# Flamingo block with mixture of experts on one core: tiled attention and scores, first rows loaded first, and a reordered second normalisation

## The reference

```python
x = x + tanh(g_xattn[0]) * xattn(layernorm(x), ctx_512, Wq, Wkv_expand, Wout)
x = x + tanh(g_ffn[0]) * ffn(layernorm(x), gate_w, w1, w2, w3, ws1, ws2, ws3)
# xattn: 16 heads of 32; scores * 1/sqrt(32), where(tril(512 x 64)), softmax over 64 keys, attn @ v, @ Wout.T
# ffn: shared expert (silu(x ws1) * (x ws3)) ws2 for every row, plus the best 2 of 8 experts, weighted by
#      softmax(x gate_w), each (silu(x w1[e]) * (x w3[e])) w2[e], inner width 256
```

## Time and profile before

| | |
|---|---|
| time, median of 3 runs (lowest, highest) | 488.65 us (487.75, 490.65) |
| time of the profiled execution | 488.76 us |
| its span, first to last instruction | 487.0 us |
| mean granted TensorE clock | 0.981 of full |
| HBM read, written | 35.54 MB, 22.70 MB |
| copy of one tile's scores (ScalarE, L713, two instructions) | 1.25 us |
| VectorE row maximum or row sum of a tile (L1088, L1094); reciprocal (L1097) | 1.21 us; 0.25 us |
| ScalarE and VectorE parts of one half of the shared weights | 1.47 us; 1.75 us |
| VectorE low part of the query weights | 2.28 us |
| ScalarE normalisation of a tile (L688), fill of kbd (4 instructions) | 0.80 us, 2.58 us |

### The profile page before, as it was taken

How to read it: one execution, slowest core, us unless ns; L and a number is a source line. 1 busy time by engine, 2 the same in 40 slices (tenths; PEclk the granted TensorE clock), 3 DMA queues, 4 the chain that set the end, 5 groups by cost and what they waited for, 6 DMA issues and landing times.

```text
span 487.0 us, 7654 instructions
## 1 busy us (share of the span) xinstructions
PE 427.6 (88%) x2445; PEld 231.1 (47%) x2446; DVE 307.9 (63%) x659; ACT 249.9 (51%) x450; POOL 230.0 (47%) x205
## 2 busy tenths in 40 slices
PE   2599789998999989988897979889999999999981
PEld 1355435554555555554444435445455545544540
DVE  4788876888568885688767868963334334333330
ACT  3879565767537675376342526743343434343330
POOL 4007527541875417749152041855546455565422
PEclk9999989999999999999998899999999999999996
DMA  7920023241042253541642375866557656576453
GB/s 305 416 69 1 0 66 126 92 153 65 2 131 86 88 194 24 173 153 67 232 193 71 107 228 167 185 122 105 116 95 125 113 102 125 88 128 104 90 66 43
DMA packets 20478, 58.61 MB, mean 120 GB/s; under 512 B 3489, under 2 KB 3745, under 8 KB 19810
## 3 DMA queue, kind: packets, MB, share of 16 engines
q0 software_dynamic: 9504, 20.48, 23.7%
q1 hardware_dynamic: 10946, 37.77, 22.9%
HBM read 35.54 MB, written 22.70 MB: 120 GB/s over the span
## 4 chain that ended last, share of the span: by engine, by line
PE 66%; DVE 15%; ACT 6%; issue 5%; POOL 3%; DMA 3%; POOLq 0%; SPq 0%; DVEq 0%; ACTq 0%
PE bank L1554 56%; PE bank L1559 9%; ACT arena L656 4%; DVE arena L987 3%; DVE xn L1056 2%; POOL arena L555 2%; DVE x_sb L1034 1%; DMA xrows<-xn 1%; DVE mx L1094 1%; DMA rows<-xrows,entry 1%; DVE mv L1002 1%; DMA arena<-in_wkv 1%; POOL lists L533 1%; ACT arena L688 1%; DVE mx L1088 1%
## 5 line engine op out<-in xcount | busy, mean ns | idle before, releaser
L1554 PE MATMUL bank<-arena 128*128 128x512 f16 (+1 forms) x576 | 109.5, 347 | 3.4 <-DVE arena L987 1.6
L1554 PE MATMUL bank<-arena,GT 128*128 x468 | 107.4, 379 | 2.2 <-issue 2.0
L640 POOL DMA_INDIRECT out<-rows,entry x39 | 61.7, 1582 | 80.8 <-ACT rows L962 29.9
L1554 PE MATMUL bank<-arena,gT 128*128 (+1 forms) x330 | 80.2, 379 | 2.2 <-DVE gT L986 1.8
L1554 PEld LDWEIGHTS bank<-arena 128*128 128x128 f16 x576 | 55.9, 98 | 51.7 <-issue 3.9
L656 ACT ACTIVATE arena<-bank 128x512 f16<-128x512 f32 (+1 forms) x88 | 49.4, 586 | 47.8 <-PE bank L1554 29.1
L1554 PEld LDWEIGHTS bank<-arena,GT 128*128 128x128 f16 x468 | 45.8, 98 | 49.0 <-issue 2.9
L987 DVE SCALAR_TENSOR_TENSOR arena<-bank,arena 128x512 f16<-128x512 f32 (+1 forms) x72 | 45.8, 666 | 22.2 <-ACT arena L656 21.8
L616 POOL DMA_INDIRECT rows<-xrows,entry x39 | 39.3, 1008 | 37.0 <-DVE entry L1362 20.3
L986 DVE TENSOR_TENSOR GT<-bank,GT 128x512 f16<-128x512 f32 x39 | 26.9, 690 | 46.4 <-ACT GT L656 46.3
L1554 PE MATMUL bank<-arena,x2T 128*128 128x512 f16 x192 | 46.6, 395 | 4.1 <-DVE x2T L986 4.1
(11 more groups left out here) (169 smaller groups left out, 590.2 us busy)
## 6 DMA issues: line engine op xcount, KB each, us to landing
x_sb<-in_experts SPq DMA_DIRECT2D x9, 768.0 KB, 5.1
rows<-in_experts SPq DMA_DIRECT2D x6, 768.0 KB, 5.7
xrows<-xn SPq DMA_DIRECT2D x16, 256.0 KB, 2.4
out<-x_sb SPq DMA_DIRECT2D x16, 256.0 KB, 2.2
image<-GT SPq DMA_DIRECT2D x5, 768.0 KB, 4.1
arena<-image SPq DMA_DIRECT2D x10, 384.0 KB, 5.3
x_sb<-in_x SPq DMA_DIRECT2D x2, 1024.0 KB, 8.8
x_sb<-in_x SPq DMA_DIRECT2D x1, 2048.0 KB, 16.3
```

Of the source, the lines that this page charges most:

```text
L640: nc.gpsimd.indirect_dma_start(out=out, out_offset=bass.IndirectOffsetOnAxis(ap=entry[:, 1, j:j + 1], axis=0), in_=Y[:, j % RING, :], in_o ...
L1554: last = nc.tensor.matmul(dst, a, b, start=n == 0, stop=n == len(steps) - 1)
```

## The change

Loads come in another order: the first two tiles of rows, the next two, then the query weights in two halves, then the context. VectorE normalises the first batch itself (`first_norm`); ScalarE did. Keys are made between the second and the third query projection, in the banks of scores and turned tiles.

`scores` uses 64 partitions (2 heads) per matmul, alternately the lower and the upper half, each half with its own bank, 24 matmuls of 128 columns per tile. `attend` takes the values where they lie, 64 keys by 32 columns per head, and writes each head to its own 32 output partitions: 48 matmuls of 512 columns per batch. vbd, its memset and `fill_v` go. `scores` waits until both halves of the previous tile are copied.

The turn of normalised tile 0 moves from the feed-forward to between the third and fourth output projection, and in the feed-forward the hidden products and the last scores change places. On GpSimd the image subtractions move behind later steps, and `softmax_sub` 2 comes after the second `power2`. On VectorE `head_max` 0 goes ahead of `make_x1` 0, the router's placement and `head_sum` 2 ahead of the mix, and shared weights, gate and aggregates of the start move. ScalarE's list follows.

```diff
-        kbd = part(NG * GH * SK, F16)
+        kbd = part(NG * 2 * SK, F16)
+        part(NG * 2 * SK)
         S = part(PER * NH * SK)
...
-        vbd = sb("vbd", [P, 2 * PR * P], F16)
...
-        wqv = wq_s.rearrange("p (h c n) -> p h c n", h=2, c=DC)
+        wqv = wq_s.rearrange("p (h g c n) -> p h g c n", h=2, g=NG, c=DC)
...
-        vbdv = vbd[:, :].rearrange("p (h r m) -> p h r m", h=2, r=PR)
...

-        MIX_FIRST = (("q", 0), ("q", 1), ("v", 0), ("q", 2), ("v", 1), ("q", 3), ("p", 0), ("v", 2), ("p", 1),
-                     ("v", 3), ("p", 2), ("p", 3))
+        MIX_FIRST = (("q", 0), ("q", 1), ("v", 0), ("q", 2), ("p", 0), ("v", 1), ("q", 3), ("p", 1), ("v", 2),
...
             return () if isinstance(b, int) and b == B - 1 else MIX
+
+        def wq_half(n, low=0):
+
+            return slice((2 * low + n) * (DC * D // 2), (2 * low + n + 1) * (DC * D // 2))
+
+        def keys_bank(g):
+
+            return (score_bank + turn_bank)[g][:, 0:B * SK]
+
+        def pair_of(g, j):
+
+            return j // 2 * NG + g
...

         @block.sync
         def _(sp):
+            for n in range(2):
+                sp.dma_start(x_sb[:, 2 * n * D:2 * (n + 1) * D].rearrange("p (t d) -> p t d", t=2),
+                             x[:, 2 * n:2 * (n + 1), :]).then_inc(ld_x0[n], 16)
+            for n in range(2):
+                sp.dma_start(wq_raw[:, wq_half(n)], wq[:, wq_half(n)]).then_inc(ld_wq[n], 16)
             sp.dma_start(ctx_raw.rearrange("p (b e k) -> p b e k", b=B, e=2), ctx_rows).then_inc(ld_kv, 16)
             sp.dma_start(wkv_raw, wkv).then_inc(ld_kv, 16)
-            sp.dma_start(x_sb[:, 0:PER * D].rearrange("p (t d) -> p t d", t=PER), x[:, 0:PER, :]).then_inc(ld_x0, 16)
-            sp.dma_start(gl[:, 0:2], gates).then_inc(ld_gates, 16)
-            sp.dma_start(wq_raw, wq).then_inc(ld_wq, 16)
             sp.dma_start(x_sb[:, PER * D:2 * PER * D].rearrange("p (t d) -> p t d", t=PER),
                          x[:, PER:2 * PER, :]).then_inc(ld_x1, 16)
...
             pool.memset(kbd.bitcast(F32), 0.0).then_inc(consts, 1)
-            pool.memset(vbd[:, :].bitcast(F32), 0.0).then_inc(consts, 1)
             pool.iota(first_high[:, :], pattern=[[-1, E]], base=E, channel_multiplier=0,
...
                     split_piece(0)
-                elif prev is not None:
-                    image_rest(2 * b - 1)
                 for i in range(PER):
                     if not nxt and i == 3:
                         split_piece(1)
+                    if nxt and prev is not None and i == 2:
+                        image_rest(2 * b - 1)
                     softmax_mul(b, i)
...
                     scatter_pairs(prev, (0,))
                 if nxt:
                     softmax_mask(b + 1)
-                    image_rest(2 * b)
                     softmax_sub(b + 1, 0)
                 power2(b, 0)
                 if nxt:
                     softmax_sub(b + 1, 1)
-                    softmax_sub(b + 1, 2)
+                    image_rest(2 * b)
                 else:
                     scatter_pairs(prev, (1,))
                 power2(b, 1)
+                if nxt:
+                    softmax_sub(b + 1, 2)

...
-                    last = hi(kbdv[rows, :, :, n * SK:(n + 1) * SK],
+                    last = hi(kbdv[rows, :, :, n % 2 * SK:(n % 2 + 1) * SK],
...
+            def wq_high(n):
+                act.wait_ge(ld_wq[n], 16)
+                hi(wq_s[:, wq_half(n)], wq_raw[:, wq_half(n)], S_W).then_inc(wq_hi, 1)
...
                 c = f + 1
-                turn_hi(c, "x2", 0)
+                turn_hi(c, "x2", 1)
+                tanh_h(f, 0)
                 scores_out(c, 3)
-                turn_hi(c, "x2", 1)
+                turn_hi(c, "x2", 2)
                 exps(c, 2)
+                tanh_h(f, 1)
+                turn_hi(c, "x2", 3)
+                turn_hi(c, "g", 0)
                 if nxt:
                     image_high(2 * c - 1)
+                    exps(c, 3)
+                    norm1(f + 2, 0)
                 else:
                     direct_hi(0)
-                tanh_h(f, 0)
-                turn_hi(c, "x2", 2)
-                turn_hi(c, "x2", 3)
-                if nxt:
-                    image_scale(2 * c - 1)
-                else:
+                    exps(c, 3)
                     direct_scale(0)
-                tanh_h(f, 1)
-                turn_hi(c, "g", 0)
-                exps(c, 3)
-                if nxt:
-                    norm1(f + 2, 0)
-                    norm1(f + 2, 1)
-                fill_v(c, (0, 1))
                 tanh_h(f, 2)
-                fill_v(c, (2, 3))
                 between(0)
                 turn_hi(c, "g", 1)
-                if not nxt:
+                router_exp(f)
+                if nxt:
+                    norm1(f + 2, 1)
+                    norm1(f + 2, 2)
+                else:
                     direct_hi(1)
                     direct_scale(1)
-                router_exp(f)
-                if nxt:
-                    norm1(f + 2, 2)
-                    norm1(f + 2, 3)
                 tanh_h(f, 3)
                 for i in range(1, PER):
                     between(i)
+                    if nxt and i == 1:
+                        norm1(f + 2, 3)
                     if i < 3:
                         turn_hi(c, "g", i + 1)
+                    if nxt and i == 2:
+                        image_scale(2 * c - 1)
                 between(PER)
                 if nxt:
                     fill_k(f + 2)
...
-                        if prev is not None and n == 1:
+                        if prev is not None and n == 2:
                             image_high(2 * b)
-                        if prev is not None and n == 2:
+                        if prev is not None and n == 3:
                             image_scale(2 * b)
...
                 if nxt:
                     scores_out(b + 1, 0)
                     if prev is None:
+                        shared_hi_half(1)
+                    scores_out(b + 1, 1)
+                    if prev is None:
                         image_high(0)
-                        image_scale(0)
-                    scores_out(b + 1, 1)
                     exps(b + 1, 0)
                     scores_out(b + 1, 2)
+                    turn_hi(b + 1, "x2", 0)
+                    if prev is None:
+                        image_scale(0)
                     exps(b + 1, 1)
                 else:
                     copy_weights(prev)
                     for k in range(7, 10):
                         split_piece(k)
+                    turn_hi(b + 1, "x2", 0)
...
+            def first_norm():
+
+                dve.wait_ge(ln1_power, 1)
+                for i in range(PER):
+                    V.tensor_scalar(xn1[:, i * D:(i + 1) * D], x_tile(i), ln1[:, i, 0:1], ln1[:, i, 2:3],
+                                    ALU.subtract, ALU.mult).then_inc(xn1_ready, 1)
...
-            dve.wait_ge(ld_x0, 16)
-            statistics1(range(PER))
+            dve.wait_ge(ld_x0[0], 16)
+            statistics1(range(2))
+            dve.wait_ge(ld_x0[1], 16)
+            statistics1(range(2, PER))
             aggregate1(0)
-            bias1(0)
...
+            own_block()
+            first_norm()
+            wq_low(0)
...
             def after_attention(f):

                 c = f + 1
-                if not isinstance(f, int) or f < B - 1:
-                    turn_lo(c, "x2", 0)
                 statistics2(f, 3)
                 aggregate2(f, 1)
                 turn_lo(c, "x2", 1)
@@ -1218,11 +1248,11 @@

                 c = f + 1
                 after_attention(f)
+                hidden(f, 0)
                 head_max(c, 3)
-                hidden(f, 0)
                 turn_lo(c, "x2", 2)
+                hidden(f, 1)
                 turn_lo(c, "x2", 3)
-                hidden(f, 1)
                 turn_lo(c, "g", 0)
                 head_sum(c, 0)
                 head_sum(c, 1)
...
             def iteration(b, prev, nxt):
                 if prev is None:
                     head_max(b, 3)
+                    aggregate1(2)
+                    head_sum(b, 0)
                 else:
                     feed_forward(prev, nxt)
+                    if nxt:
+                        router_place(prev)
+                        head_sum(b, 2)
                 for kind, n in mix(b):
                     if kind == "q":
                         project_lo(b + 1, n)
-                        if prev is None:
-                            head_sum(b, n)
+                        if prev is None and n < 2:
+                            head_sum(b, n + 1)
                     elif kind == "v":
                         values_lo(n)
+                        if n == 0:
+                            head_sum(b, 3)
                     else:
                         probabilities_lo(b, n)
                         if prev is not None and n == 0:
-                            head_sum(b, 2)
```

(82 more changed lines are left out.)

157 lines of the change are left out of this document (79 added, 78 removed).

## The result

The changed kernel takes 500.3 us (median of 4 runs, 497.0 to 501.7) against 488.2 us before (median of 4). The ratio of the means is 1.023, 95% interval 1.019 to 1.027: 11 us slower, where 8 us less were forecast. The profiled execution took 497.04 us, with a span of 495.3; its counterpart is the 487.0 of before.

The account below looks back on a forecast made before the run. TensorE, busy 88% of the span, and its waits were taken as the bound. Gains of 4.0 + 0.2 + 2 x 0.4 + 2 x 1.0 + 1.2 = 8.2 us brought 488.76 to 480.5 us, range 467 to 491.

Parts of the forecast that it names:

- Where that goes: Batch boundary: TensorE idles some 2.4 us for normalised rows; 3.1 us gain shrinks to 0.4, bounds -1.0 and +2.5.
- Tiled attention and scores: TensorE: attention's matmuls fall from 5.2 to 2.6 us per batch, scores from 1.31 to 0.65 us per tile.
- Rivals 1 and 2: Attention: tiles take turns, 514 us, chance 0.10 (1); only pairs run together, attention 5.2 us, 491 us, chance 0.12 (2).
- Rival 4: Tiled stretches: array must empty at each entry and exit, 0.17 us each, up to 6.7 us, 487 us; chance 0.05.
- The chain of the second normalisation: Batch boundary: GpSimd's subtractions hold VectorE's normalisations over 2 us twice per batch; TensorE waits some 2.4 us.
- Rival 3: Second normalisation: GpSimd does not hold up VectorE, each of four pairs ends 1.9 us sooner, 471 us; chance 0.19.
- boundary and mix together: Between attentions: boundary gain 0.2 us in batch 0, 0.4 in batches 1 and 2, plus 1.0 us per mix.
- The mix: Last mix of a batch: router placement and tile 2's sum first, net gain 1.0 us per batch, for two batches.
- The start: Up to batch 0's attention: projection at 16.7 instead of 21.4 us, attention at 60.3 instead of 64.34; gain 4.0 us.
- Smaller edits: Scores waiting for both halves of the copy cost nothing; in batch 0 at most 0.6 us.
- The last feed-forward but one: Feed-forward before the last batch's attention: a gain of 0.3 us, counted within the last batch's 1.2.

Follow-up runs that it names:

- tiled_alone: The kernel before with only the changed kernel's tiled attention and scores (`fill_v` and vbd gone), everything else in the old order: 499.8 us, ratio 1.0173.
- no_scatters: The changed kernel without the sixteen scatters of batches 0 and 1 and the waits on them: 491.1 us, ratio 1.0037.
- start_alone: The kernel before with the new loads, start and first batch alone; untiled, second normalisation as before, nothing filled: 490.8 us, ratio 1.0026.
- combined: Changed kernel, second normalisation's old order, products ahead of the split, 23 empty matmuls at the start, second four scatters in the next batch's feed-forward: 487.7 us, 0.9960.
- after_untiled: The changed kernel with attention and scores untiled as before (`fill_v` back); new loads, start and orders kept: 495.2 us, ratio 1.0142.
- scatters_split: The changed kernel with the eight scatters in two fours, the second behind the subtraction of tile 0: 499.6 us, ratio 1.0247.
- combined_filled: The combined kernel with some 70 more empty matmuls in TensorE's remaining waits: 483.8 us, ratio 0.9873.
- combined_mix: combined_filled with the changed kernel's VectorE order ahead of the mix (router placement and row sum of tile 2 first): 479.8 us, ratio 0.9809.
- before_scatters_late: The kernel before, untiled, with only the eight scatters of batches 1 and 2 moved behind the second power of the normalisation: 502.4 us, ratio 1.0283.

## Why the prediction was wrong

**The step that failed** is the first of "Where that goes" and the sum behind it: every idle time of TensorE was charged at its own length, and TensorE's work at the full clock, so that the worst that it allowed at a batch boundary was a loss of 1.0 us. The runs show two costs in its place. (a) Beside the eight scatters the tiled matmuls starve: 5.4 and 5.8 us instead of 2.8, in that kernel. (b) Idle times, those of the stalls and those that the sum itself names, can be followed by the lower clock, with full matmuls at twice their time. Not every one is: behind the wait of 1.78 us at 147.45 in the changed kernel the full matmuls run at full speed. Filling the waits for the normalised rows alone gives back 6 us, taking the scatters away 9 us of both costs together; tiled_alone shows that they outweigh what the tiling gains. Between attention 1 and 2 the account closes: 5.9 us for the stall and what follows it at the lower clock, less 1.7 gained elsewhere, is the 4.2 lost. None of the rivals had either; the trace of before held a hint of (b), the 0.80 of the earlier trace rows behind a wait of 2.08 us, which the text used for that one attention only.

**Tiled attention and scores**: right. 2.6 and 0.65 us were forecast, less the 0.17 us of a lone matmul; less the same 0.17, the runs of 2.77 and 0.84 us are 2.60 and 0.67. 48 x 0.215 = 10.3 us in turn against 2.60 is a factor of 4.0. The Trainium skill, "TensorE: Matmul & The Clock Gate", section "Measured speedup vs the span model", has 3.07 for four row tiles; with tiles of 64 rows and 32 columns, four in a row on different columns, the measurement is better, and decides. Rivals 1 and 2 fall: there is no turn-taking. Rival 4 is there, at a little over half its price. The starts in no_scatters show it:

```profile
118.73 2.75 PE L1591 MATMUL bank<-arena 128*128 128x512 f16 x12
121.32 1.04 PE L1596 MATMUL bank<-ident,arena 128*128 128x128 f32 x8
122.19 2.75 PE L1591 MATMUL bank<-arena 128*128 128x512 f16 x12
124.87 2.77 PE L1725 MATMUL bank<-arena 64*32 64x512 f16 x48
127.58 0.84 PE L1713 MATMUL bank<-arena 64*128 64x128 f16 x24
```

Twelve full matmuls take 2.59 us to the next start where a whole-array turn follows and 2.68 where attention does; attention's 2.60 become 2.71 to the scores, and the scores' 0.67 become 0.78 to the next full matmul (131.77 to 132.55). Each change of the tile's shape thus costs 0.1 us where rival 4 took 0.17. For some 37 changes that is 3.7 us of TensorE's time, an estimate, part of it in waits that are there anyway.

**The chain of the second normalisation**: right in kind. TensorE was to stand 2.4 us ahead of the first turn; it stood 2.66, 1.78 and 1.79. The normalised rows were to be held by GpSimd. The instructions of that line, beside the earlier trace rows (shortest, median, longest in ns):

```profile
L1094 DVE TENSOR_SCALAR xn<-x_sb,ln x16: 534/840/2115, 79.9 to 271.3; 128x512 f32<-128x512 f32 x16
```

and in the timeline of batch 2's boundary, beside the earlier trace rows:

```profile
210.69 3.11 DVE L1094 TENSOR_SCALAR xn<-x_sb,ln 128x512 f32<-128x512 f32 x2 [0.92 <-POOL ln L530]
220.00 2.49 DVE L1094 TENSOR_SCALAR xn<-x_sb,ln 128x512 f32<-128x512 f32 x2 [0.30 <-POOL ln L530]
```

The median rose from 544 to 840 ns, and both pairs of a batch took over 2 us. Rival 3 falls. The forecast put the gain of boundary and mix together at 1.2 us for batch 0 to 1 and 1.4 for 1 to 2; without the scatters the distances of attention are 61.1 and 59.5 us against 62.8 and 61.2, so 1.6 and 1.7. (The first is 61.1 in the changed kernel as well, where no stall has come yet.) The mix gave what it should: its wait went from 1.50 to 0.71 us.

**The start**: mis-sized. The term was 4.0 us. The first projection began at 16.23 us as forecast (16.7), but attention of batch 0 in start_alone at 63.4, a gain of 0.9 and not 4; in the changed kernel none. Part is the clock: filled, the start reaches 61.55. The lead is lost early. In start_alone the first projection begins 5.2 us sooner than before (16.21 against 21.42), but the long run of scores and projection 0.4 us later (37.63 against 37.21), behind waits of 1.00, 0.55 and 1.57 us, two of them for VectorE's part of the turned rows. And the tiled scores of tiles 2 and 3 wait 1.17 us each for ScalarE's copy, where "Smaller edits" allowed at most 0.6:

```profile
39.88 1.46 PE L1719 MATMUL bank<-arena 64*128 64x128 f16 x24 [1.17 <-ACT arena L720]
42.52 1.46 PE L1719 MATMUL bank<-arena 64*128 64x128 f16 x24 [1.17 <-ACT arena L720]
```

And in start_alone attention of batch 1 comes at 128.4, 1.3 us later than before: TensorE waits 2.83 us for the first normalised tile of batch 0, where the kernel before has no such wait. In VectorE's order the second half of the shared weights now stands in front, for which the text took 0.2 as a gain; that this is the cause is argued from the order, no run moved it.

**The last feed-forward but one**: a missing term. The sum gave this pass a gain of 0.3 us. ScalarE scales the expert's piece behind the exponential of tile 3, GpSimd's split waits for that, and the products behind the split:

```profile
230.44 3.53 POOL L579 TENSOR_TENSOR arena<-x_sb,arena 128x384 f16<-128x384 f32 x4 [4.06 <-ACT x_sb L672]
233.93 5.62 POOL L570 TENSOR_TENSOR arena<-arena,rd 128x1024 f32<-128x1024 f32 x3
235.88 1.09 PE L1602 MATMUL bank<-ident,arena 128*128 128x128 f32 x8 [1.96 <-POOL arena L570]
...
238.50 2.60 PE L1597 MATMUL bank<-arena,gT 128*128 128x512 f16 x6
```

Before, the three products stood at

```profile
221.25 5.64 POOL L555 TENSOR_TENSOR arena<-arena,rd 128x1024 f32<-128x1024 f32 x3
```

The products start 42.6 us behind attention (before: 221.25 - 188.32 = 32.9; no_scatters: 38.4, so some 4 of these 10 us go with the scatters). TensorE waits 1.96 us, and six matmuls take 2.60 us instead of 1.46. Undoing the orders brings the distance from attention 2 to 3 from 58.4 to 54.3 us, with the products first as well (combined) to 49.2.

**How the 11 us divide**, by kernels: start +1.3 (start_alone); new orders on top, untiled, 0.0116 x 488 = +5.7 (after_untiled); tiling on top of that +4.3, which is its 8.5 us gained less about 13 lost to stalls and clock. The three depend on each other (tiled alone costs 8.5), so this is one path of several, and by the intervals the last two are good to some 3 us each.

**Left open**: what starves. In all eight tiled kernels with eight scatters in a row (the changed one among them) there were two stalls, in scatters_split, no_scatters, combined_filled and combined_mix none. The untiled ones that I looked at have at most 1.4 us, at the end of the second eight:

```profile
198.00 13.15 PE L1614 MATMUL bank<-arena 128*128 128x512 f16 x72 [1.36 <-issue]
```

That is start_alone. In the eight, stalls began 6.3 to 9.1 us after the first issue and ended 2.4 to 2.5 us after the last one began. A supply of instructions that slows while the scatters run would look like this, but nothing here shows it. If short matmuls only used it up sooner, their number should decide: the eight stalled 64 to 81 matmuls after the first issue, and before_scatters_late ran 85 and 103 beside its scatters without a stall. The trace of the changed kernel records transfers of instructions too, 30 in all, and none of them falls into either stall. The Trainium skill, "Runtime: NRT & Kernel Launch", section "Instruction fetch mechanics", says that fetching is hidden behind the rate of issue; whether the "issue" gaps are an exception to that no run here shows.

## What to carry to other kernels

A chained kernel in which TensorE already waits need not gain from less TensorE work: read the granted clock of each stretch, and reckon with matmuls at double length behind an idle time. Matmuls into a bank that nobody reads, in waits whose length is known, can keep the clock and cost nothing (59 of them gave 6 us back here). In these kernels tiling paid only once the waits were filled and the scatters split. Before making matmuls short, look what GpSimd issues beside them; and cost a reordering once for every shape of a pass, the last but one too.

## What the runs showed of the hardware

- Eight indirect DMAs issued by GpSimd in a row go with stalls of TensorE's short matmuls in the tiled kernels: 2.6 to 5 us per eight scatters, with gaps of 0.2 to 1.2 us put down to "issue"; ScalarE, which waits for them, shows "remote". Without the scatters the stalls are gone. Fours in a row did not stall them, but for 1.3 and 0.3 us in one kernel (combined, 192.93 and 240.28); nor did eight in before_scatters_late.
- The lower clock comes behind idle times (here of 1 to 7 us), not behind each, and not in the same places in each execution: 37 to 53 us of it in four executions of one program. Its cost shows as 12 full matmuls in 5.1 to 5.3 us instead of 2.75. The Trainium skill, "TensorE: Matmul & The Clock Gate", section "A second HAM failure mode: psum-queue depth-cycling", says of another kernel that a TensorE which idles briefly between groups of matmuls can swing between the levels; the traces agree.
- Four tiles of 64 rows by 32 columns, on the two halves of the rows in turn, work side by side: 48 matmuls of 512 columns in 2.77 us, 0.054 us each (less the 0.17 of a lone one) against 0.215 for one of the whole array.
- A change between the whole array and a tile shape, or between two tile shapes, costs 0.1 us (2.68 and 2.59 us for the same 12 matmuls with and without one behind them).
